# A graph layer with an expert layer: edge sums by matmuls with the node places as stationary operand, products in two fp32r parts

## What is computed

```python
h = layernorm(x)
m = clifford_linear(h[src] * r[edge_type], msg_w, msg_b)     # 256x256 matrix
m = m * sigmoid(r[edge_type] @ gate_w.T + gate_b)
m = m * max(deg_src[src] * deg_dst[dst], 1) ** -0.5
h_agg = segment_sum(m, dst)
x = x + clifford_linear(h + h_agg, upd_w, upd_b)
n = layernorm(x); w = softmax(mean(n, axis=0) @ Wr + br)     # one "batch" row: per node
for e in range(8):                                            # 8 experts, all used
    y_e = relu(bn2(relu(bn1(n @ W1[e])) @ W2[e])) @ Wo[e] + bo[e]
x = x + sum_e w_e * y_e
```

## Time and profile before

| | |
|---|---|
| median of 3 runs | 1954.49 us (1953.44 to 1954.67) |
| the profiled execution | 1955.06 us, its span 1953.0 us |
| PE busy | 1869.2 us, 96% of the span |
| POOL busy | 1399.4 us, 72% |
| ACT busy | 1005.7 us, 51% |
| DVE busy | 787.6 us, 40% |
| chain that ended last | PE 87%, POOL 5%, DVE 3%, issue 3% |

### The profile page before, as it was taken

The page is one execution under the profiler, slowest core; times in us unless marked ns, Lnnn a source line. Parts: engine busy times, 40 slices in busy tenths (PEclk is TensorE's granted clock), DMA queues, the critical chain, the costliest instruction groups (busy, mean ns, idle before and its releaser), DMA issues.

```text
span 1953.0 us, 35233 instructions
## 1 busy us (share of the span) xinstructions
PE 1869.2 (96%) x13045; PEld 1690.8 (87%) x13046; DVE 787.6 (40%) x1834; ACT 1005.7 (51%) x2286; POOL 1399.4 (72%) x1410
## 2 busy tenths in 40 slices
PE   6848988999999999999999999999999999999998
PEld 6837887988998998998998998998998998998888
DVE  8953332333333334343343343333333343333342
ACT  6444644545555555555555555554554554553445
POOL 4877777777777777777777777777777777777600
PEclk9968989999999999999999999999999999999999
DMA  8185444434434434444444443443443443444400
GB/s 244 52 292 176 125 114 117 125 106 127 121 103 127 123 103 125 125 108 121 125 113 116 126 123 105 126 123 103 126 124 104 125 125 103 125 112 108 93 12 6
DMA packets 91761, 232.32 MB, mean 119 GB/s; under 512 B 24748, under 2 KB 39210, under 8 KB 91679
## 3 DMA queue, kind: packets, MB, share of 16 engines
q0 software_dynamic: 66336, 184.06, 35.5%
q1 hardware_dynamic: 24528, 46.21, 7.2%
q10 hardware_dynamic: 815, 1.16, 0.2%
HBM read 217.90 MB, written 13.44 MB: 118 GB/s over the span
## 4 chain that ended last, share of the span: by engine, by line
PE 87%; POOL 5%; DVE 3%; issue 3%; DMA 1%; ACT 1%; DVEq 0%; POOLq 0%; SPq 0%
PE z L755 34%; PE y L785 17%; PE agg L800 17%; PE pr L809 9%; POOL H L405 3%; PE y L731 3%; PE y L722 2%; POOL R L405 2%; DVE H L939 2%; PE y L677 2%; PE z L707 1%; PE y L743 1%; PE y L723 1%; PE y L777 1%; ACT big L508 1%
## 5 line engine op out<-in xcount | busy, mean ns | idle before, releaser
L405 POOL DMA_INDIRECT H<-h_table,src x784 | 770.8, 983 | 238.9 <-issue 236.5
L405 POOL DMA_INDIRECT R<-r_table,typ x598 | 615.3, 1029 | 199.2 <-issue 197.9
L593 ACT ACTIVATE h<-z,bns 128x256 f32<-128x256 f32 (+1 forms) x864 | 417.3, 539 | 627.1 <-PE z L755 624.6
L1144 DVE SCALAR_TENSOR_TENSOR acc<-y,wg,acc 128x256 f32<-128x256 f32 x392 | 173.4, 479 | 699.8 <-PE y L785 699.7
L800 PE MATMUL agg<-S,H 128*86 128x64 f32 x4704 | 398.5, 242 | 0.7 <-issue 0.7
L800 PEld LDWEIGHTS agg<-S,H 128*86 128x86 f32 x4704 | 394.5, 160 | 2.0 <-issue 1.2
L755 PE MATMUL z<-hT,big 128*128 128x256 f32 (+1 forms) x1728 | 385.2, 366 | 1.9 <-ACT h L593 1.9
L785 PE MATMUL y<-big,h 128*128 128x256 f32 x1568 | 378.2, 382 | 1.7 <-DVE lg L1107 1.6
L755 PE MATMUL z<-h,big 128*128 128x256 f32 (+1 forms) x1728 | 375.5, 360 | 0.4
L755 PEld LDWEIGHTS z<-h,big 128*128 128x128 f32 x1728 | 304.9, 190 | 36.8 <-ACT h L593 1.0
L785 PEld LDWEIGHTS y<-big,h 128*128 128x128 f32 x1568 | 291.3, 190 | 42.1 <-issue 1.9
(11 more groups left out here) (162 smaller groups left out, 1070.7 us busy)
## 6 DMA issues: line engine op xcount, KB each, us to landing
H<-h_table,src POOLq DMA_INDIRECT x784, 2.8
tb<-in_typ_row SPq DMA_DIRECT2D x24, 448.0 KB
R<-r_table,typ POOLq DMA_INDIRECT x598, 2.8
h_table<-big SPq DMA_DIRECT2D x7, 910.0 KB, 8.8
big<-in_x SPq DMA_DIRECT2D x7, 896.0 KB, 10.9
big<-in_w SPq DMA_DIRECT2D x8, 768.0 KB, 4.8
acc<-in_x SPq DMA_DIRECT2D x22, 256.0 KB, 5.4
out<-acc SPq DMA_DIRECT2D x22, 256.0 KB
```

What stands on the lines that cost most here:

```text
L405: pool.indirect_dma_start(out=to[:, b * DX:(b + 1) * DX], out_offset=None, in_=tab, in_offset=bass.IndirectOffsetOnAxis(ap=ix[:, J * SB + ...
L593: last = s_.activation(o[:, m, 0:wide_], z_[:, m, 0:wide_], ACT.Relu, bias=bns[:, l, 1, c:c + 1], scale=bns[:, l, 0, c:c + 1])
L1144: last = v.scalar_tensor_tensor(out=acc[:, g % 3, t, :], in0=b[:, t * D:(t + 1) * D], scalar=wg[:, t, e_:e_ + 1], in1=acc[:, g % 3, t, :], ...
```

## The change

**Sums.** The one-hot `S` becomes the stationary operand (128 edges x 128 places, the node's number mod 128) and the products the moving one, in two fp32r parts: ACT copies the products of an sb to `HI` (`high_act`, 128x1040), DVE subtracts to `LO` (128x1040), and TensorE runs 8 fp32r matmuls of 258 columns per sb into one of two PSUM banks `O`, which two sbs (a pair) fill. DVE adds a bank to `sums` of the two tiles that it may touch, under a mask (`take_dve`, two instructions of 128x258 per pair). `AGG`, `carry_act`, `zero`, `sums` and the column load go. The sums now lie with the nodes on the partitions, so TensorE transposes them (`at_pe`, 2 transposes per tile behind s4, copied by ACT), and `x2_pe` (2 matmuls of 256 columns per tile) moves behind s5; the message bias is added by DVE.

**Relation blocks.** Of two sbs' 8 blocks TensorE reads 3 instead of 2: one for an even sb, two for an odd one; 505 blocks are gathered instead of 598. `PR` has two banks, the one-hots three buffers.

**Order.** DVE makes the products of J+2 and then the low parts of J+1 ahead of them; ACT makes the one-hots of J+3, and the high parts of J+2 between the two activations of the next step. The rings are NH = 6 and RB = 38; POOL gathers `H` of J when `LO` of J-6 is made, 38 `R` gathers come first. The groups end at even sbs.

The parts of the diff below are, in order, the sums on TensorE, the loop of `rel_pe`, the high parts and their place in ACT's `ffn`, the low parts and the order on DVE, and POOL's wait.

```diff
-                    col = pe.value_load(base_i[0:1, ds(J, 1)], min_val=0, max_val=512 - W)
-                    pe.wait_ge(prod, J + 1)
-                    if not isinstance(J, int) or J + 1 < WHOLE:
-                        rel_pe(J + 1, j + 1)
+                def sb_pe(i, j):
+                    if not isinstance(i, int) or j + 2 < WHOLE:
+                        rel_pe(i, j + 2)
+                    pe.wait_ge(lo_ready, i * (2 * STEP) + (j + 1))
+                    if j % 2 == 0 and j > 2:
+                        pe.wait_ge(o_free, i * STEP + (j // 2 - 1))
                     for b in range(SB):
-                        for m in range(3):
-                            last = pe.matmul(AGG[0:M3, m, ds(col, W)], H[:, j % NH, b * DX + m * M3:b * DX + (m + 1) * M3],
-                                             S[:, j % 2, b, :], start=False, stop=True, skip_group_check=True)
+                        for x in (HI, LO):
+                            last = pe.matmul(O[:, j // 2 % 2, 0:D + 2], S[:, j % 2, b, :], x[:, j % 2, b * DX:b * DX + D + 2],
+                                             start=j % 2 == b == 0 and x is HI, stop=j % 2 == 1 and b == SB - 1 and x is LO)
                     last.then_inc(mm, 1)
...
+                    for q, b in read_blocks(j, max(WHOLE, j + 1)):
+                        pe.wait_ge(oh_t, i * (3 * STEP) + (q + 1))
+                        if j:
+                            pe.wait_ge(prod, i * (2 * STEP) + j)
...
+                def high_act(J):
...
+                    act.wait_ge(prod, J + 1)
+                    if J > 1:
+                        act.wait_ge(mm, J - 1)
+                    s_.activation(HI[:, J % 2, :], H[:, J % NH, :], ACT.Copy).then_inc(hi_ready, 1)
...
                                 layer(0, s, h1[:, s % 2, :, :], wide[g])
+                            between()
                             if 0 < s <= NE:
...
+                def low_dve(J):
...
+                    if J > 1:
+                        dve.wait_ge(mm, J - 1)
+                    v.tensor_tensor(S[:, J % 2, :, :], dloc[:, J * SB:(J + 1) * SB].unsqueeze(2).to_broadcast([P, SB, P]),
+                                    iota_w[:, 0:P].unsqueeze(1).to_broadcast([P, SB, P]), ALU.is_equal)
+                    dve.wait_ge(hi_ready, J + 1)
+                    h_ = H[:, J % NH, :]
+                    v.tensor_tensor(LO[:, J % 2, :], h_, HI[:, J % 2, :].bitcast(fp32), ALU.subtract).then_inc(lo_ready, 1)
...
+                def sb_dve(some):
+                    for J in some:
+                        take_dve(J)
+                        low_dve(J + 1)
+                        prod_dve(J + 2)
...
-                        pool.wait_ge(mm, J - NH + 1)
+                        pool.wait_ge(lo_ready, J - NH + 1)
```

More of the change, by code:

```diff
@@ L37, in sizes, with edges @@
         t += w
[L38 to L44, removed]
+    def edges(t, sign):
+        p = min(1.0, t * P / n)
+        return e * p + sign * 5.5 * sqrt(e * p * (1 - p))
+    done = [min(nsb, 2 * ceil(edges(t + 1, 1) / (2 * SE))) for t in range(nt)]
+    needed = [done[t0 + w - 1] for t0, w in groups]
+    twos = [g for g, (t0, w) in enumerate(groups) if w == 2]
+    step = max(2, round(P * e / (n * SE)) * 2)
+    lead = max([needed[g] - step * (groups[g][0] + 2) // 2 for g in twos] + [2])
     ends = []
@@ L47, in sizes, with read_blocks @@
         end = step * (t0 + 2) // 2 + lead if w == 2 else needed[g]
-        ends.append(min(nsb, max([end, 1] + ends[-1:])))
+        ends.append(min(nsb, max([end, 2] + ends[-1:])))
     ends[-1] = nsb
+    tiles = []
+    for j in range(nsb // 2):
+        lo = min(sum(done[t] <= 2 * j for t in range(nt)), nt - 1)
+        hi = max([t for t in range(nt) if edges(t, -1) < (2 * j + 2) * SE] + [lo])
+        tiles.append((lo, hi))
     assert n < nt * P
-    whole = ends[pairs[-1]] if pairs else nsb
-    alike = [g for g in pairs if g + 2 in pairs and ends[g + 1] - ends[g] == step == ends[g + 2] - ends[g + 1]]
+    whole = ends[twos[-1]] if twos else nsb
+    alike = [g for g in twos if g + 2 in twos and ends[g + 1] - ends[g] == step == ends[g + 2] - ends[g + 1]]
     loop = range(alike[0], alike[-1] + 1) if alike else range(0)
-    return nt, nsb, groups, ends, step, loop, whole
+    loop = loop[:len(loop) // 2 * 2]
+    return nt, nsb, groups, ends, step, loop, whole, tiles
+def read_blocks(j, whole):
+    return [] if j >= whole else [(3 * (j // 2) + i + j % 2, SB - 1 - j % 2 + i) for i in range(1 + j % 2)]
 def ring(nsb, whole):
@@ L154, in build @@
         dd = sb("dd", [P, 2])
+        gs = sb("gs", [P, 2])
         st = sb("st", [P, 2, 6])
@@ L1089, in x2_dve @@
                         dve.wait_ge(y_free, no + YS)
+                        for t in range(nt):
+                            x_ = acc[:, g % 3, t, :]
+                            last = v.scalar_tensor_tensor(out=x_, in0=mbias[:, :], scalar=gs[:, t:t + 1], in1=x_,
+                                                          op0=ALU.mult, op1=ALU.add)
+                        link(last)
                         for t in range(nt):
```

529 lines of the change are left out of this document (309 added, 220 removed).

## The result

The changed kernel takes **1968.23 us** (median of 4 runs, 1967.58 to 1969.22), beside 1953.97 for the kernel before: a ratio of 1.0074, interval [1.0057, 1.0092]. The forecast was 1938, faster. The profiled execution has a span of 1966.5 us.

What follows compares the result with a forecast made beforehand. PE and POOL were taken to bound the kernel together. The loop's 20 x (-3.6 + 3.0 + 0.6) = 0, start -8 and end -8 took the profiled 1955.06 to 1939, median 1938 us; range 1880 to 1972.

Steps and rivals of the forecast that it cites:

- The start, -8: Start: with 38 R gathers ahead instead of 45, the first H gather comes 8.7 us earlier, at 117.5; -8 us.
- The longer way from products to sums costs one step once: Ramp: the longer way costs one step once, 0 to +5 us, left out of the sum.
- POOL's smaller need: Ramp, where POOL paces PE until about sb 26: fewer gathers give 0 to -5 us, left out of the sum.
- The loop, 72.1 us a group: Loop: -3.6 us of PE work, +3.0 of waits, +0.6 of clock per group; 20 groups sum to 0.
- PE's work: Loop, per pair group: sums -6.96, relation blocks +3.80, x2 -0.87, transposes +0.44; 68.5 instead of 72.08 us.
- The walk's waits: PE, s8 to s1: waits of 0.65 and 0.35 us for DVE, 1.7 for ACT; s5 0.25; 3.0 us given back.
- The clock, +0.6 a group: Loop: the 1.7 us wait lowers PE's clock in one group of three, losing 1.7 us each time; 0.6 a group.
- The end, -8: End: 10 sbs without relation blocks save 0.87 us each; -8 us.
- POOL, 8.6 us an sb: Gathers: 6.43 per sb at 1.25 us, plus surplus beside DVE instructions; 8.5 to 9.1 us an sb, 8.6 taken.
- the last rival: POOL shut out wholly by every DVE instruction with two SBUF inputs: 86 us a group, some 2220 us; chance 0.02.
- The one that gave 1961 to 1977: Rival: the wait behind s1 passes 2 us, the clock falls in every group, 73.2 to 74 us; chance 0.19.
- The general path: Rival: the test of the nodes' spread fails, all sbs run for each group, many times the time; chance 0.01.

Runs made afterwards that it cites:

- e8: Changed kernel with TensorE's relation sums of J+2 placed behind the edge sums of J: 1969.67 us, 1.0094 of the kernel before.
- e7: Changed kernel with DVE's low-part subtraction cut from 1040 to 8 columns, PE multiplying HI a second time: 1942.28 us, 0.9941 of the kernel before.
- f1: Changed kernel with the look-ahead of products and high parts taken back up to sb 34: 2023.80 us, 1.0358 of the kernel before.
- f4: Changed kernel, e8's order on PE, low parts of J, products of J+1 and ACT's rounding one sb nearer the gathers up to sb 34: 2067.11 us, 1.0572.
- e2: Changed kernel with ACT's normalised tile made behind s7 of the group before instead of behind s0: 1951.06 us, 0.9989 of the kernel before.
- e3: Changed kernel with DVE making the products of J+2 before the low parts of J+1: 1967.22 us, 1.0079 of the kernel before.
- e1: Changed kernel with two relation blocks at the even sbs and one at the odd ones: 1980.70 us, 1.0136 of the kernel before.
- e4: Changed kernel with the edits of e1, e2 and e3 together: 1942.38 us, 0.9946 of the kernel before.
- e5: Changed kernel with TensorE's program written out for all groups, no loop on TensorE: 1966.99 us, 1.0076 of the kernel before.
- e6: Changed kernel with the edits of e2, e3 and e5 together: 1942.98 us, 0.9947 of the kernel before.
- f3: Changed kernel with e6's loop behind f1's ramp: 1975.88 us, 1.0109 of the kernel before.
- f7: Changed kernel with the edits of e4 and e5 together: 1947.22 us, 0.9968 of the kernel before.
- f6: Changed kernel with f4's and e6's edits, and one-hot S built by four DVE operations with one SBUF tensor and a scalar: 2051.16 us, 1.0497.

## Why the prediction was wrong

- **The start, -8: this step failed.** I read the 4.24 us of the chain's piece as the landing of the last store of `h_table`. The piece is only what the chain kept of it. The rows above show that the stores last until 126 (before, 125): the 45 `R` gathers of before had covered them to within a us, and 38 leave POOL idle for 7.5 us. A saving was counted in front of a transfer that ended at the same time.
- **"The longer way from products to sums costs one step once": named, and left out of the sum; this term failed too.** It is the ramp's +9. I set it against POOL's smaller need (0 to -5), of which the ramp shows nothing. These two points are 17 us of the 30 between 1938 and 1968. That it is one sb's period is read from the two pairs of rows; e8 excludes PE's order, e7 shows that the ramp moves with the gathers while the way from gather to sums stays longer, f1 and f4 show that my two ways to give the look-ahead back cost more. No run removed it alone: that the look-ahead is its cause is argued, and its 8.9 us rest on the traces.
- **The loop, 72.1 us a group: right, by parts partly wrong.** Measured 72.27. Sums of an sb 0.95 to 0.96, relation blocks +3.72, sums -6.86, x2 -0.8: as worked out. PE's work came to 69.0 (72.27 less 3.25 of waits by start distances) instead of 68.5. The walk's waits were 0.65, 0.35, 1.7 and 0.25, in sum 3.0; measured 0.82, 0.21, 1.80 and 0.42, in sum 3.25, at those places and with those releasers. e2 and e3 confirm the two main ones by removing them: 1.0 us a group each.
- **The clock, +0.6 a group: wrong.** It is 1.00 in the groups from 540 to 1763, with waits of 1.6 us. That this error and the half us of PE's work cancelled is luck.
- **Not foreseen: PE's back edge.** +5 us at the loop's entry here; in e1, e2, e3, e4, e8 and f4 1.7 to 3.7 us idle at irregular passes. The kernel before, with half the body, shows none. The queue of kind `instruction` goes with it: over the whole execution it moved 26 packets before, 34 after and in e7 with one such idle time, 42 in e2 with two, 51 in e4 and e8 with three, 79 in f4 with six, 105 in e3 with nine, and 82 where PE's program is written out (e5, e6, f3, f7). As I read it, PE's program was being loaded again in those passes; why in those and not in others stays open.
- **The end, -8: measured -3.** 3.30 us before a turn at 1880.37, again released by ACT's L632, took a part, and from 1879.4 on 6.8 us at a granted clock of 0.50 another (an estimate, half of the 5.8 us that PE was busy in them: 2.9).
- **POOL, 8.6 us an sb: a little low.** It issued at 8.8 to 8.9, its old pace, with fewer gathers. By the lines of e7 the surplus in the loop was 0.67 us an sb (6.46 gathers of 1.05 us instead of 0.95), for the 0.55 that I took, inside my bounds (0.5 to 1.0). In the loop as changed it costs nothing; it is what stopped e6 and f7. No run shows the 86 us a group of the last rival; 0.67 of the 2.77 us of such DVE operations came on top. The Trainium skill (SBUF — State Buffer, section "Who interferes with whom") says that a DVE instruction with two SBUF inputs contends with a GpSimd instruction that reads SBUF, and that the lock is exclusive. The trace agrees for gathers, which read their row numbers from SBUF, where they start within such an instruction: 201 of those 229 took over 1.0 us. A gather that had started first was not held up, which is why the price is a quarter and not the whole.
- **The rivals.** The one that gave 1961 to 1977 has the right time for a wrong reason: no clock fell in the groups. e7 shows what it would have taken: with waits of 2.0 us the clock fell in 4 of 17 groups, not in each. The general path wasn't taken.

## What to carry to other kernels

Before a saving at the start of a stage is counted, find what else must have landed there: a queue that is exactly covered by another has nothing to give. A new stage between a gather and its use lengthens the way through the ramp even if no engine is full: here by about one period of the slowest producer, once. And where two engines bound a kernel together, take a step's work from one only with something for the other: the sums alone were 5% slower, with the relation block 0.7%, and with ACT's and DVE's order mended (e4, e6) 0.5% faster.

## What was not expected of the hardware

- A gather on GpSimd is held up by a DVE operation with two SBUF tensors as inputs if it starts while that operation runs, and then ends 0.82 us behind its end; one that started before it takes 0.95 us as ever. In the changed kernel 201 of the 229 gathers that started so took over 1.0 us, and none of the other 658. An operation with one SBUF input and one in PSUM held none (`H<-H,pr`: 49 gathers started beside it, `acc<-y`: 69), and one with an SBUF tensor and a scalar next to none (f6). In all it was 0.24 us for each us of such operations.
- TensorE stood 1.7 to 3.7 us without a releaser at the back edge of a loop whose body was two groups, in some passes and not in others, each time with some nine packets in the queue of kind `instruction`, and in none of the straight code of e5, e6, f3 or f7.
- Waits of 1.6 to 1.8 us in each group (the changed kernel, e5, e8) brought no stretch at the lower of the clock's two levels (granted 0.50, 1.2 GHz). Of waits and idle times of 1.7 to 3.7 us at the turn (e7) and at the back edge some were followed by 3.4 or 6.8 us at that level, others not.
- Chips differ: on one the kernel before took 22% longer (2392 us), and the three kernels run there and elsewhere stood 2.6 to 3.9 points worse against it than on the others.
